# Row scatters of the second batch without a TensorE wait, and a shared sum moved between two orders on VectorE

## What is computed

```python
def _L1_ffn_ref(hidden_states, gate_w, wg, wu, wd, sg, su, sd):
    x = hidden_states.reshape(-1, HID)                       # 2048 tokens, 256
    scores = jax.nn.sigmoid(x @ gate_w)                      # 32 experts
    topk_w, topk_i = jax.lax.top_k(scores, TOP_K)            # six of them
    topk_w = topk_w / (jnp.sum(topk_w, axis=-1, keepdims=True) + 1e-20)
    combine = jnp.sum(jax.nn.one_hot(topk_i, N_EXP, dtype=topk_w.dtype) * topk_w[..., None], axis=1)
    g = jnp.einsum('td,edf->tef', x, wg)
    u = jnp.einsum('td,edf->tef', x, wu)
    act = jax.nn.silu(g) * u
    routed = jnp.einsum('tef,efd,te->td', act, wd, combine)
    shared = jax.nn.silu(hidden_states @ sg) * (hidden_states @ su) @ sd
    return routed + shared
...
x = _layernorm(x + _L1_ffn_ref(x, ...), axis=-1)
```

## Time and profile before

| | us |
|---|---|
| median of 3 runs | 1553.4 |
| lowest and highest | 1550.3, 1554.28 |
| the profiled execution's own time | 1552.69 |
| its span from first to last instruction | 1550.9 |
| PE, DVE busy | 1307.6, 1040.1 |
| ACT, POOL busy | 878.3, 681.5 |

### The profile page before, as it was taken

The page is one execution under the profiler, slowest core; times in us unless marked ns, Lnnn a source line. Parts: engine busy times, 40 slices in busy tenths (PEclk is TensorE's granted clock), DMA queues, the critical chain, the costliest instruction groups (busy, mean ns, idle before and its releaser), DMA issues.

```text
span 1550.9 us, 26467 instructions
## 1 busy us (share of the span) xinstructions
PE 1307.6 (84%) x9434; PEld 830.2 (54%) x9434; DVE 1040.1 (67%) x2748; ACT 878.3 (57%) x1244; POOL 681.5 (44%) x862
## 2 busy tenths in 40 slices
PE   6477756776789999689999898999999978799995
PEld 5233443333567877434444544444444445699984
DVE  7757697768443366868777576777988256355685
ACT  3578627877442343347777575666777641366660
POOL 8477254657201104213233742432237627666661
PEclk9599986998999999669899999989999979899998
DMA  2690000013302101000000000000004445577875
GB/s 94 227 362 15 1 1 1 1 48 99 102 11 72 42 14 43 0 1 1 2 1 1 1 1 1 2 1 1 1 18 162 166 183 175 184 212 213 264 258 224
DMA packets 69143, 124.40 MB, mean 80 GB/s; under 512 B 7318, under 2 KB 55190, under 8 KB 67992
## 3 DMA queue, kind: packets, MB, share of 16 engines
q1 hardware_dynamic: 56728, 85.99, 17.3%
q0 software_dynamic: 12288, 36.72, 6.3%
HBM read 60.29 MB, written 62.39 MB: 79 GB/s over the span
## 4 chain that ended last, share of the span: by engine, by line
PE 53%; DVE 24%; ACT 10%; POOL 6%; issue 4%; DMA 2%; SPq 0%; POOLq 0%; DVEq 0%; ACTq 0%
PE psum L2459 10%; PE psum L2345 8%; PE psum L2434 7%; PE psum L2665 6%; DVE psum L3057 5%; PE psum L2564 4%; DVE probs L3077 3%; PE psum L2688 3%; ACT probs L2790 3%; PE psum L2406 3%; PE psum L2585 3%; POOL many_x L3778 2%; PE psum L2448 2%; DVE neg_max L3060 2%; PE psum L362 2%
## 5 line engine op out<-in xcount | busy, mean ns | idle before, releaser
L2788 ACT ACTIVATE probs<-psum,exp_shift 128x1024 f32<-128x1024 f32 (+1 forms) x320 | 325.6, 1031 | 147.9 <-PE psum L2434 143.7
L3057 DVE CUSTOM_DVE_ANT_0 psum<-psum,stage 128x512 f32<-128x512 f32 (+3 forms) x512 | 288.6, 618 | 86.1 <-PE psum L2406 86.0
L3714 POOL TENSOR_SCALAR_AFFINE_SELECT probs<-probs 128x512 f32<-128x512 f32 x192 | 140.3, 742 | 369.9 <-ACT probs L2788 267.7
L2434 PE MATMUL psum<-qt,kt 32*128 32x512 f32 (+5 forms) x1152 | 240.3, 451 | 53.2 <-ACT probs L2790 19.8
L2406 PE MATMUL psum<-kt,qt 32*128 32x512 f32 (+3 forms) x768 | 208.5, 455 | 21.5 <-DVE neg_max L3057 15.1
L3077 DVE TENSOR_TENSOR probs<-probs 128x1024 f32<-128x1024 f32 (+1 forms) x136 | 169.6, 1291 | 63.0 <-ACT probs L2790 62.8
L2434 PEld LDWEIGHTS psum<-qt,kt 32*128 32x128 f32 (+1 forms) x1152 | 106.6, 198 | 194.6 <-issue 77.5
L2459 PE MATMUL psum<-probs,v 128*32 128x256 f32 (+3 forms) x2048 | 178.2, 447 | 1.9 <-POOL probs L3714 1.9
L3785 POOL DMA_INDIRECT results<-sp_y,sp_row x128 | 125.9, 984 | 60.1 <-ACT sp_y L2849 32.3
L2790 ACT ACTIVATE probs<-psum 128x1024 f32<-128x1024 f32 (+1 forms) x160 | 140.5, 947 | 7.4 <-PE psum L2434 7.4
L3060 DVE TENSOR_REDUCE neg_max<-psum 128x1 f32<-128x256 f32 (+3 forms) x256 | 111.1, 484 | 30.7 <-PE psum L2406 30.5
(11 more groups left out here) (362 smaller groups left out, 2585.4 us busy)
## 6 DMA issues: line engine op xcount, KB each, us to landing
many_x<-blank SPq DMA_DIRECT2D x2, 10240.0 KB, 50.6
sp_xs<-many_x SPq DMA_DIRECT2D x64, 320.0 KB, 3.9
sp_w<-in_sparse SPq DMA_DIRECT2D x8, 1280.0 KB, 10.0
x_turned<-results SPq DMA_DIRECT2D x8, 768.0 KB, 7.2
sp_back<-results SPq DMA_DIRECT2D x8, 768.0 KB, 10.6
sorted_x<-blank SPq DMA_DIRECT2D x2, 1152.0 KB, 6.5
sorted_y<-y SPq DMA_DIRECT2D x18, 128.0 KB, 1.7
rows<-in_x SPq DMA_DIRECT2D x4, 512.0 KB, 7.1
```

Source lines behind the costliest of these rows:

```text
L2434: inst = pe.matmul(psum[:, base - early:base + QCH - q0], A.kt[rows, k_slot, key * P:(key + 1) * P], A.qt[rows, q_slot, c * QCH + q0 - ear ...
L2788: inst = act.activation(dst, view, ACT.Exp, bias=exp_shift[:, 0:1])
L3057: inst = dve.tensor_tensor_reduce(src, src, causal_bf[:, (4 - cols) * P:4 * P], -1.0, -MASKED, ALU.add, ALU.min, dst)
L3714: pool.affine_select(out=dst, in_=dst, compare_op=ALU.is_ge, fill=0.0, base=0, pattern=[[0, 4], [1, P]], channel_multiplier=-1).then_inc(p ...
```

## The change

- The scatters of parts 1 and 2 no longer carry `latest["PE"]`; they wait for `where` and for the cleared tensor alone. Those of part 0 keep it.
- All scatters that are still to be recorded when the shared expert ends are recorded there, and the call in the loop over the pairs is gone: none stands behind a result on GpSimd.
- In `amid_last`, `shared_gates(0, 1)` and `shared_mult(0, 1)` are recorded ahead of the logits of part 1, no longer behind its `slots`.
- Half of the `weigh` steps that are still due come after the step `by_token` of part 1, no longer ahead of it.
- In `plan_sparse`, `go_on` of part 1 and `shared_add(0)` come ahead of the turns of part 2's tokens, and in that order; they stood behind `by_token`.

```diff
@@ plan_second_attention
                 ending = amid()
                 next(ending)
+                for _ in range(2):
+                    weigh()
+                next(ending)
                 while due:
                     weigh()
-                next(ending)
                 normalize_half(1, 1)
@@ plan_many_route
-                            scatter_singly=[lambda i=i: scatter(i, 1, (latest["PE"],))
+                            scatter_singly=[lambda i=i: scatter(i, 1, () if part else (latest["PE"],))
                                             for i in range(t0 * TOP_K, (t0 + n) * TOP_K)])
@@ amid_last
                 route = middle["route"]
+                shared_gates(0, 1)
+                shared_mult(0, 1)
                 route["logits"](take_pair, give_pair)
...
                 to_scatter.extend(route["scatter_singly"])
-                shared_gates(0, 1)
                 scatter_some(2)
-                shared_mult(0, 1)
                 yield
@@ plan_sparse
                 scale()
+                route1["go_on"]()
+                shared_add(0, start)
                 for part in route["turn"]:
                     part(take_pair, give_pair)
                 scatter_some(2)
                 route["logits"](take_pair, give_pair)
                 scatter_some(2)
                 route["by_token"](take_pair, give_pair)
-                shared_add(0, start)
-                route1["go_on"]()
                 shared_gates(1, 0)
...
                         shared_mult(*steps[n])
+                scatter_some(len(to_scatter))
@@ loop over the pairs
                     gates(p)
-                    scatter_some(2)
                     if p >= 1:
```

## The result

The changed kernel takes 1544.05 us in the median of 8 runs (1539.96 to 1547.5), the kernel before 1552.29 (1548.25 to 1556.42): a ratio of 0.9938, 95% interval 0.9917 to 0.9959, so 8.2 us faster. The forecast was 1540.5 with a range of 1537 to 1545. The profiled execution took 1543.04 us (span 1541.3), against 1552.69 (1550.9) before: 9.6 us less, where the sum had 12.7.

A forecast was written before the change was run, and what follows sets the result against it. The last GpSimd scatter was taken to hold up pair 8 on TensorE, and so the end. 9.7 us from scatters plus 3.0 from the clock made 12.7 us, giving a median of 1540.5 us, range 1537 to 1545.

The forecast's parts named there:

- Scatters: GpSimd, parts 1 and 2: first scatter at 1264.6, 1.27 us a step, last at 1324.3 against 1334.02, 9.7 us earlier.
- rival 1: GpSimd's scatters are slower unpaced, 1.38 us a step: 5.2 us less gain, 1545.7 us; chance 0.09.
- Landing and load: After the last scatter: 2.48 us landing and 2.97 us load of pair 8's rows, carried over unchanged.
- Where the clock comes back: TensorE, first three pairs from pair 8: no half clock after a shorter stall, 3.0 us gained, bounds 0 to 3.0.
- signs of being wrong: Changed profile: first scatter behind 1266, steps over 1.3 us, clock 0.50 after 1330, or GpSimd still behind at last pair.
- Rival 3: TensorE's clock falls after the short stall too: 3.0 us less gain, 1543.5 us; chance 0.07.
- Shared half (0,1) ahead of the logits: TensorE's four matmuls fit the 1.83 us gap at 1246.72; ScalarE's two table loads still allow `ranks` transposed at 1250.2.
- rival 2: Part 1's routing is 2.8 us later through ScalarE's two table loads: 1543.3 us; chance 0.09.
- The output projection: TensorE, behind the moved matmuls: starts 2.7 us earlier, partly at low clock, ends some 1.3 us earlier, near 1264.2.
- rival 4: TensorE bounds because the stall before pair 8 goes: at most 2.5 us more gain, 1538 or 1537 us; chance 0.05.
- rival 5: GpSimd's results bound the pairs from 1.52 us a step on, eating the gain; 1563 us at 1.60; chance 0.02.
- Rival 6: Another wait, for experts' loads or `sp_xs`, takes its place at 1329.8: gain under 4.7 us, 1550 us; chance 0.04.

The follow-up runs named there:

- experiment 1: Kernel before with the scatter edits alone (no TensorE wait, all recorded ahead of the pairs), old order kept: 1540.02 us, ratio 0.9915.
- experiment 2: Changed kernel with the scatter edits undone, the moves in order kept: 1550.77 us, ratio 0.9963 to the kernel before.
- experiment 10: Changed kernel without the last four of part 2's scatters, output wrong, on a chip like the first: 1540.48 us, ratio 0.9911 to before.
- experiment 3: Kernel before with only the TensorE wait of the second batch's scatters removed, their places kept: 1546.87 us, ratio 0.9976.
- second profile: Both kernels run again unchanged on another chip like the first; the changed kernel took 1542.27 us, ratio 0.9924 to before.
- experiment 4: Changed kernel with 14 identity products on TensorE ahead of its wait for pair 8's rows: 1539.16 us, ratio 0.9891 to before.
- experiment 11: Kernel before with the scatter edits alone plus six identity products ahead of TensorE's wait for pair 8's rows: 1544.11 us, ratio 0.9931.

## Why the prediction was right, and where its sum was off

- **The mechanism held.** Scatters bound pair 8, pair 8 bounds the end. Experiments 1 and 2 put the whole gain on the scatters' edits, and experiment 10 got the further 5.8 us that the same reading gives.
- **Scatters: 9.7 us earlier forecast, 9.4 measured** (1334.02 to 1324.59; by `where`, 69.93 to 60.61). The first started at 1264.92 and not 1264.6: I had added 0.30 us to the end of `where`, it is 0.94 behind its start in every profile from chips like the first without the wait. The pace was 1.27, as taken; rival 1 (1.38) did not come. The split between the waits and the two results held (2.6 by experiment 3, forecast 2.5).
- **Landing and load: 5.45 us taken, 7.01 measured** (3.89 + 3.12). I had carried over a single row, without a range. The second profile has 5.52, but landings in an unbroken row of scatters spread over 1.4 us, and are 0.7 longer in the mean. Here 1.6 of the missing 3.3 us went.
- **"Where the clock comes back": the mis-sized term.** I took all 3.0 us; the profile gave 1.3 (the first three pairs lost 3.03 us to the pace before, 1.76 or 1.77 after). Of the signs of being wrong that the prediction names, one came: a clock of 0.50 after 1330 (0.57 in the mean of 1332 to 1336). Two things failed. The row at 1292.22, eight matmuls at full clock after 2.26 us idle, did not speak for this place, nor even for its own: in after the same eight take 3.10 us behind 2.28 us idle, and behind the waits for pair 8 of 1.54, 2.65, 4.04 and 4.38 us the clock fell each time. And not all of the 3.0 would have come back even at full clock: the first pair then still costs 1.0 to 1.4 us more than the pace (experiments 4 and 11), for the loads of the expert numbers behind the wait. Rival 3 was thus half right, and its 0.07 too small.
- **Added up:** 9.4 - 1.6 + 1.3 = 9.1 of the 9.4 us that the ruler shows, where the forecast had 12.7. (Two slips of 0.1 stand in the forecast's own sum: 1552.69 - 12.7 is 1540.0, and with 0.7 it is 1540.7, not 1540.5.) That the median came out inside the range owes something to the range: it allowed for rival 3, of which about half came. For the second pair of profiles: 69.91 - 60.54 = 9.4, landing and load -0.1, the clock 0.4 (3.01 us lost before, 2.61 after): 9.7 of 9.6.
- **Shared half (0,1) ahead of the logits.** It fitted the gap (1.88 us from 1244.97, at full clock), the two table loads cost what was taken (1.28 us each), and `ranks` of part 1 was transposed at 1250.46, forecast 1250.2. The transpose was 0.3 us later than before, and `where` didn't move (1263.98, 1264.09 before). In ScalarE's timeline there is still no drain:

```profile
1246.93 1.28 ACT L2860 ACT_TABLE_LOAD   x1
1248.23 0.59 ACT L2860 ACTIVATE s_silu<-psum 64x512 f32<-64x512 f32 x1
1248.84 1.28 ACT L2828 ACT_TABLE_LOAD   x1
1250.13 0.28 ACT L2828 ACTIVATE ranks<-psum 128x128 f32<-128x128 f32 x1
```

  The silu starts 0.02 us behind its load, and the load starts 0.01 us behind the ACTIVATE ahead. The Trainium skill (ScalarE: Activation LUTs, What ACT_TABLE_LOAD costs) would add a drain to each load; the measurement decides, rival 2 stayed away.
- **The output projection: wrong, and without consequence.** It was to end near 1264.2; it ended at 1266.27. I had doubled 1.5 us of it for the low clock, but all of it ran low: its products start at 1257.85 with 0.41 us where 0.28 is the full clock's, and the stretches show it (the earlier trace rows had 1.00 for the same four us):

```profile
1260.00:1262.00 2.00, 2.00 (x8) 1.57 (x7) 1.75 (x8) 0.00 (x0) 0.72 (x1) 0.50 0.98 389
1264.00:1268.00 4.00, 4.00 (x12) 3.15 (x12) 1.75 (x4) 0.00 (x0) 2.47 (x3) 0.50 1.02 429
```

  So VectorE's L3100 came at 1266.37, 0.7 later than before instead of 1.4 earlier. The gate products that moved away had been what TensorE worked off at the low clock: in both profiles of before and in experiments 1 and 11 they come first, and the projection behind them runs at full clock from its second product on; in both profiles of after the projection comes first and all of it is slow. Later waits gave it back: TensorE was ready for pair 8 at 1327.61, forecast 1327.3, so the end saw nothing of it.
- **Rivals 4, 5 and 6.** The wait for the rows did not go, so TensorE did not bound. GpSimd caught up with the results by 1339.10, where it first waited for a result again (0.86 us), and the steps stayed at 1.27. Rival 6 did not come on chips like the first. On the other chip something near it did, by a cause that no profile of before could show: cover for pair 8's rows from a late start of the pairs.
- **The median.** The sum made against one profiled execution was carried over whole; the profiles' gains of 9.4 and 9.6 us stand beside 8.2 and 9.8 between medians.

## What to carry to other kernels

A wait that is taken from a chain gives at most the chain's own time, and what an engine loses behind its stall can have two parts. One is what its sequencer had yet to do behind the wait, here register loads that otherwise lie under running matmuls; look for it in the engine's queue before you blame the engine that the row names. The other is the clock, which a few idle products ahead of the wait held up here, with no gain that a median or the ruler could tell. The longer of the two counts where they overlap. Where executions differ by more than the edit is worth, measure between two rows of the same profile that enclose the edit, repeat the profile to see how far the ruler itself moves, and use the medians to confirm the sign. A step that takes the tail of one queue off the critical path is worth nothing where something else is later, so look for the cover on each chip before counting the gain as general.

## What the runs showed of the hardware that was not expected

- The same short idleness left TensorE's clock up in one order and not in the other. Ahead of part 1's last shared products (L2607 before, L2609 after) TensorE stands 2.25 to 2.69 us in the five profiles with before's order and 2.26 to 2.30 us in the five with the new one. The eight products behind it take 1.99 or 2.00 us in each of the five, and 3.08 to 3.19 us in each of the others. In before the clock had fallen near 1274 (0.50 in 1276 to 1280) and was back at 1.00 by 1284; in after it had been at 1.00 without a break from 1272. That this is the cause is not shown. Ahead of pair 8 it fell after waits from 1.54 us on, though in the case of 1.54 us the first eight matmuls still ran at full clock and the slow ones began 2.1 us behind the end of the wait.
- In experiment 1 the gate products began at 1257.03 and the clock was 0.50 until 1260 and 0.99 in 1260 to 1262; in after the projection's products began at 1257.85 and the clock stayed at 0.50 until 1268.
- Behind a wait at full clock TensorE stood 0.6 to 1.0 us ahead of its next matmuls with a register load of 0.57 to 0.74 us in its queue (experiments 1, 4, 11 and after's second profile).
- The landing of an indirect scatter of 128 rows: 2.48 us in each of four profiles in which the scatter of the same kind ahead of it was three steps back, 2.48 to 3.89 in five in which it was one step back.
- One of the four chips of the experiments ran the kernel before 3.4% slower than the first result had it; the four kernels profiled there have stretches of up to 19.4 us in which ScalarE or VectorE waits for nothing that the trace shows.
